# Attention with 8-wide heads: maximum products dealt one by one between scores and values, and another order of stores and loads in the first round

## What is computed

```python
x = x + _L1_attn_ref(_layernorm(x, axis=-1), ...)      # fifth branch
...
x = x + _L3_attn_ref(_layernorm(x, axis=-1), ...)      # eleventh branch

def _L1_attn_ref(x, wq, bq, wk, bk, wv, bv, wo, bo):
    q, k, v = (proj(wq, bq), proj(wk, bk), proj(wv, bv))   # 16 heads x 8
    scores = jnp.einsum('bhqd,bhkd->bhqk', q, k) * scale
    attn = jax.nn.softmax(scores, axis=-1)
    out = jnp.einsum('bhqk,bhkd->bhqd', attn, v)
    ...
    return jnp.einsum('bld,ed->ble', out, wo) + bo

def _L3_attn_ref(x, Wq, bq, Wk, bk, Wv, bv, Wp, bp, rel_bias_table):
    # as above, with rotary q and k, and before the softmax:
    att = (jnp.einsum('bhid,bhjd->bhij', q, k) + bias[None]) * (1.0 / math.sqrt(D))
    att = jnp.where(pos[None, :] <= pos[:, None], att, -jnp.inf)
```

## Time and profile before

| | us | share of the span |
|---|---|---|
| median of three runs | 3683.9 | |
| the profiled execution, its own time | 3683.4 | |
| its span | 3681.6 | 100% |
| PE busy | 3164.9 | 86% |
| PEld busy | 1625.1 | 44% |
| DVE busy | 2543.4 | 69% |
| ACT busy | 1894.4 | 51% |
| POOL busy | 1013.4 | 28% |

### The profile page before, as it was taken

One profiled execution on the slowest core, in us unless ns is written; L12 is line 12 of the kernel. 1 busy time (PEld: TensorE's weight loads), 2 busy tenths in 40 slices (PEclk: granted clock), 3 DMA queues, 4 the chain that ended last, 5 costly groups with the idle time before them and its releaser, 6 DMA issues. The chain is left out here.

```text
span 3681.6 us, 61554 instructions
## 1 busy us (share of the span) xinstructions
PE 3164.9 (86%) x23589; PEld 1625.1 (44%) x23629; DVE 2543.4 (69%) x5604; ACT 1894.4 (51%) x3454; POOL 1013.4 (28%) x860
## 2 busy tenths in 40 slices
PE   4678876799979999999889988989998688788899
PEld 3212233566642222222356666656675222222577
DVE  8787779877858888888477774464434777884433
ACT  2232222677747888888677773223222256667321
POOL 0345552767730000000187650001201201211100
PEclk9879978899988999999999999989999579899899
DMA  0000000211124000000021100001101400000100
GB/s 21 9 1 1 0 0 12 75 28 33 31 75 172 1 1 1 2 1 1 26 58 37 31 20 28 2 26 45 49 1 50 123 1 30 33 1 1 45 1 12
DMA packets 72696, 99.85 MB, mean 27 GB/s; under 512 B 11668, under 2 KB 50968, under 8 KB 72280
## 3 DMA queue, kind: packets, MB, share of 16 engines
q1 hardware_dynamic: 72408, 95.92, 8.8%
HBM read 60.18 MB, written 19.45 MB: 22 GB/s over the span
## 5 line engine op out<-in xcount | busy, mean ns | idle before, releaser
L1958 ACT ACTIVATE AR<-ps 128x1024 f32<-128x1024 f32 (+2 forms) x756 | 716.5, 997 | 175.4 <-PE ps L1861 142.0
L2041 DVE TENSOR_REDUCE AR<-ps 128x1 f32<-128x512 f32 x1056 | 689.4, 687 | 144.5 <-PE ps L1829 131.6
L1861 PE MATMUL ps<-AR 32*128 32x512 bf16 (+3 forms) x4992 | 511.9, 382 | 6.2 <-ACT AR L1958 3.1
L1829 PE MATMUL ps<-AR 32*128 32x512 bf16 (+3 forms) x1664 | 362.6, 400 | 117.9 <-DVE AR L2038 59.7
L1878 PE MATMUL ps<-AR 128*32 128x512 f32 (+3 forms) x3328 | 444.9, 608 | 5.7 <-ACT AR L1963 5.2
L2464 PEld LDWEIGHTS ps<-AR 128*128 128x128 f32 x3072 | 363.0, 192 | 60.5 <-issue 47.6
L2623 DVE SCALAR_TENSOR_TENSOR X<-ps,AR,X 128x128 f32<-128x128 f32 x512 | 143.6, 344 | 343.9 <-PE ps L2464 343.6
L2464 PE MATMUL ps<-AR 128*128 128x128 f32 x3072 | 363.2, 275 | 0.0
L1829 PEld LDWEIGHTS ps<-AR 32*128 32x128 bf16 x1664 | 94.9, 92 | 504.1 <-DVE AR L2041 241.2
L2439 PE MATMUL ps<-XT,AR 128*128 128x512 f32 x672 | 307.7, 594 | 0.1
L209 POOL TENSOR_TENSOR rs<-rs,halves 128x4 f32<-128x4 f32 x48 | 49.5, 1032 | 818.1 <-DVE rs L201 818.0
(11 more groups left out here) (324 smaller groups left out, 5718.9 us busy)
## 6 DMA issues: line engine op xcount, KB each, us to landing
AR<-AR SPq DMA_DIRECT2D x124, 128.0 KB, 2.3
AR<-in_c_rot SPq DMA_DIRECT2D x64, 128.0 KB, 2.2
AR<-in_L3f_w SPq DMA_DIRECT2D x30, 256.0 KB, 5.2
rows_KA<-AR SPq DMA_DIRECT2D x32, 128.0 KB, 2.4
AR<-scr_bias SPq DMA_DIRECT2D x32, 128.0 KB, 3.2
AR<-in_L2f_w SPq DMA_DIRECT2D x30, 128.0 KB, 2.7
AR<-rows_KC SPq DMA_DIRECT2D x7, 512.0 KB, 6.2
AR<-rows_KA SPq DMA_DIRECT2D x6, 512.0 KB, 5.1
```

The lines of the kernel that those rows point to most:

```text
L1829: e.matmul(g.bank[b][:, 0:w], QA[rows, q, 128 * i:128 * i + 128], KA[rows, q, 512 * first:512 * first + w], start=way != "kept", stop=True ...
L1861: t = e.matmul(g.bank[h][:, lo:512], K[32 * h:32 * h + 32, q, 128 * kt:128 * kt + 128], Q[32 * h:32 * h + 32, q, queries], start=y == 0, s ...
L1958: e.activation(dst[:, :, lo:512], src[:, :, lo:512], ACT.Exp, scale=self.scale).then_inc(*s.up("exp" if u else "left", k, i, *((1,) if u e ...
L2041: e.tensor_reduce(o, g.bank[b][:, 0:w], AXX, ALU.max).then_inc(*s.up("reduced", k, n, h, st, kc))
```

## The change

- **Dealing.** The maximum products of a step come one head at a time instead of in pairs of heads: with four of them, one ahead of the first scores, one between the first and the second scores, one between the second scores and V, one behind V. With more, they are spread over the four slots evenly. The scores of a step thus become two entries of the list, "score" 0 and 1; "step" remains for the engines that read it.
- **Closing.** The closing of a round stands at the end of a step, behind V and the fourth slot, instead of ahead of a finish and V.
- **Head.** "kept" and "met" go to head 1 instead of head 3.
- **Fills.** The five constant blocks are copied from a new input, `c_fill`, by five DMAs at the start of the kernel, behind the loads of X and of c_mats and ahead of the first stage's loads. The buffer, the two memsets of GpSimd and the five DMAs in the non-causal stage are gone.
- **First round.** Chunk 2 of q is made ahead of chunks 0 and 1; it is stored and loaded alone ahead of these two; chunks 0 and 1 have a signal of their own, `d_loaded7`.
- **Table.** After the last piece, ScalarE takes an exponential of one column (`warm`), in both stages.

```diff
+    c["c_fill"] = np.stack([np.full((128, 1024), 0x3F803F80, np.uint32), np.zeros((128, 1024), np.uint32)]).view(f)
...
         self.parts = [(c, j) for c in range(4) for j in (1, 0)] if causal else [
-            (0, 1), (3, 0), (1, 1), (2, 1), (3, 1), (0, 0), (1, 0), (2, 0)]
+            (0, 1), (3, 0), (1, 1), (2, 1), (3, 1), (2, 0), (0, 0), (1, 0)]
...
-        if self.causal or (n and h != 3):
+        if self.causal or (n and h != 1):
             return "alone"
...
-    def plan_max(self, n, half, st, kc):
+    def plan_max(self, n, half, st, kc, only=None):
         out = []
-        for h in (2 * half, 2 * half + 1):
+        for h in (2 * half, 2 * half + 1) if only is None else (only,):
...
             pairs = [self.next_max(half, goal, 3) for half in (1, 0)]
-            order = [x[y] for y in range(3) for x in pairs if y < len(x)]
-            if order:
-                self.plan_max(*order.pop(0))
-            self.plan.append(("step", i, n, kt, self.hold(0, ("left", i)) + self.hold(1),
-                              self.hold(2, ("exp", i, 1)) + self.hold(3)))
-            for x in order:
+            order = [x[y] + (2 * x[y][1] + z,) for y in range(3) for x in pairs if y < len(x) for z in range(2)]
+            slots = [[x for y, x in enumerate(order) if 4 * y // max(4, len(order)) == z] for z in range(4)]
+            for u in range(2):
+                for x in slots[u]:
+                    self.plan_max(*x)
+                self.plan.append(("score", i, n, kt, u, self.hold(2 * u, ("exp", i, 1) if u else ("left", i)) + self.hold(2 * u + 1)))
+            self.plan.append(("step", i, n, kt))
+            for x in slots[2]:
                 self.plan_max(*x)
             if self.rows_due:
                 self.plan_rows_max(self.rows_due.pop(0))
-            self.plan_closed()
             if finish_due:
                 self.plan_finish(finish_due.pop(0))
...
+            for x in slots[3]:
+                self.plan_max(*x)
+            self.plan_closed()
             p += area[i]
...
-            e.wait_ge(*s.at("filler", k, 1))
-            for block in (2, 3):
-                e.dma_start(g.rows["KC"][:, block, :, :], self.filler[:, 0:2048]).then_inc(*s.up("d_stored7", k, "KC", block, by=16))
-            for name, block in (("QB", 3), ("QC", 2), ("QC", 3)):
-                e.dma_start(g.rows[name][:, block, :, :], self.filler[:, 2048:4096]).then_inc(
-                    *s.up("d_stored7", k, name, block, by=16))
             self.store_all(e, s, 0, 1, chunk(0), "d_stored0")
...
             self.store_rest(e, s, 3, 1, whole, "d_stored5")
-            e.wait_ge(*s.at("third", k, 2, 0))
-            most = slice(0, 1536)
-            self.store_all(e, s, 2, 0, most, "d_stored6")
-            e.wait_ge(*s.at("d_stored7", k, "QC", 3))
+            self.store_all(e, s, 2, 0, chunk(2), "d_stored6")
+            e.wait_ge(*s.at("d_filled", "QC", 3))
             e.wait_ge(*s.at("d_stored5", k, "KC", 1, 3))
...
-            self.load(e, s, "QA", 0, most, "d_loaded6")
-            self.store_rest(e, s, 2, 0, most, "d_stored6")
-            e.wait_ge(*s.at("d_stored6", k, "QC", 1, 2))
+            self.load(e, s, "QA", 0, chunk(2), "d_loaded6")
+            self.store_all(e, s, 1, 0, slice(0, 1024), "d_stored7")
+            self.store_rest(e, s, 1, 0, slice(0, 1536), "d_stored7")
+            e.wait_ge(*s.at("d_stored7", k, "QC", 1, 1))
+            most = slice(0, 1536)
+            self.load(e, s, "QA", 0, slice(0, 1024), "d_loaded7", "a")
             self.load(e, s, "QB", 0, most, "d_loaded7", "b")
             self.load(e, s, "QC", 0, most, "d_loaded7")
...
                 e.activation(self.P[:, j, 1, chunk(c)], self.RC[:, y % 3, :], ACT.Copy).then_inc(*s.up("piece", k, c, j, 2))
+                if y == len(self.parts) - 1:
+                    e.activation(self.warm[:, 0:1], self.bqk[:, 0:1], ACT.Exp)
...
-            e.memset(self.filler[:, 0:2048], 1.0).then_inc(*s.up("filler", k, 0))
-            e.memset(self.filler[:, 2048:4096], 0.0).then_inc(*s.up("filler", k, 1))
...
     e.dma_start(g.C[:, :], g.I["c_mats"]).then_inc(*s.up("d_c", by=16))
+    for name, block, x in (("KC", 2, 0), ("KC", 3, 0), ("QB", 3, 1), ("QC", 2, 1), ("QC", 3, 1)):
+        e.dma_start(g.rows[name][:, block, :, :], g.I["c_fill"][x].bitcast(BF16).rearrange("(h d) n -> h d n", h=16)).then_inc(
+            *s.up("d_filled", name, block, by=16))
     for stage in stages:
         stage.sync(e, s)
```

More of the change, by code:

```diff
@@ L1446, in allocate @@
         self.junk = ar.bf16(2, 512)
+        self.warm = ar.f32(2)
         if causal:
@@ L1454, in allocate @@
         self.PB = ar.f32(4, 1024)
-        self.filler = self.PB.rearrange("p a b -> p (a b)").bitcast(BF16)
         assert not causal or ar.at <= 41500 - 9216
@@ L1667, in max_rows_in @@
             return "d_loaded%d" % c
-        return "d_loaded4" if c == 3 else "d_loaded6"
+        return "d_loaded4" if c == 3 else "d_loaded6" if c == 2 else "d_loaded7"
     def score_rows_in(self, gr, c, key):
@@ L1846, in tensor @@
                 t.then_inc(*s.up("m_turned", k, n))
-            if what == "step":
-                i, n, kt, old0, old1 = x
+            if what == "score":
+                i, n, kt, u, old = x
                 (gr, qc), lo = self.rounds[n], self.low(n, kt)
                 q, queries = gr % self.slots, slice(512 * qc + lo, 512 * qc + 512)
[L1851 to L1862, removed]
-                    t.then_inc(*s.up("scored", k, i, u))
+                self.wait_left(e, s, old)
+                if u == 0 and kt == 0:
+                    e.wait_ge(*s.at("max_row", k, n))
+                name = self.score_rows_in(gr, kt // 4, True)
+                if name not in seen:
+                    seen.add(name)
+                    e.wait_ge(*s.at(name, k))
+                for y, (K, Q) in enumerate(((KA, QA), (KA, QB), (KC, QC))):
+                    for h in (2 * u, 2 * u + 1):
+                        t = e.matmul(g.bank[h][:, lo:512], K[32 * h:32 * h + 32, q, 128 * kt:128 * kt + 128],
+                                     Q[32 * h:32 * h + 32, q, queries], start=y == 0, stop=y == 2, skip_group_check=True)
+                t.then_inc(*s.up("scored", k, i, u))
             if what == "values":
@@ L1938, in scalar @@
             if what == "step":
-                i, n, kt, _, _ = x
+                i, n, kt = x
                 near, lo = self.near_cols(n, kt), self.low(n, kt)
@@ L2084, in gpsimd @@
         g, k = self.g, self.k
-        if not self.causal:
-            e.memset(self.filler[:, 0:2048], 1.0).then_inc(*s.up("filler", k, 0))
-            e.memset(self.filler[:, 2048:4096], 0.0).then_inc(*s.up("filler", k, 1))
         e.memset(self.MN.rearrange("p a b c -> p (a b c)"), 0.0).then_inc(*s.up("m_cleared", k))
@@ L2667 @@
     "d_expert%d" % i for i in range(8)) + tuple("d_low%d" % i for i in range(6)) + tuple(
-        "d_loaded%d" % i for i in range(14))
+        "d_loaded%d" % i for i in range(14)) + ("d_filled",)
 SHARED = {
     "v_setup": ("halves", "identb", "cleared", "q_scale", "band", "x_cleared", "o_cleared", "masked", "offset_scale", "selection"),
-    "g_setup": ("taps_cleared", "k_padded", "v_padded", "k_cleared", "v_cleared", "m_cleared", "filler", "ones"),
+    "g_setup": ("taps_cleared", "k_padded", "v_padded", "k_cleared", "v_cleared", "m_cleared", "ones"),
     "router": ("logits", "compared", "rank", "mass", "chosen", "gates"),
```

## The result

The changed kernel takes 3650.0 us (median of four runs, 3643.0 to 3656.7) against 3683.1 before; the ratio is 0.9908, its 95% interval 0.9887 to 0.9930. It is **faster by 33 us**, where 3687 was forecast and 3666 was the lower end. The profiled execution of after took 3656.7, its span is 3654.9 against 3681.6; it is the slowest of the four.

What follows compares the result with a forecast made beforehand. First-stage steps were bound by a three-bank loop of maximum product, reduce, next products and V. Terms -9.2 + 4.5 + 6.4 - 4.5 + 3 + 2.6 = +2.8 gave 3686.2, stated as 3687; range 3666 to 3702.

Steps and rivals of the forecast that it cites:

- The step that failed: Causal stage: steps with eight or more maxima are paced by VectorE, eight reduces taking 5.1 before and after.
- Net 2.6 lost: Causal stage in sum: 2.9 gained in regular steps, 5.5 lost at finish and maximum row; bounds 8 gained, 11 lost.
- Rival 2: Causal stage: shorter TensorE waits bring a third of the low-clock time back to 2.4 GHz; 20 less, 3667; chance 0.18.
- Rival 1: First attention stage: VectorE's four reduces become the loop if over 0.65 apart; 12 slower, 3699; chance 0.18.
- The first stage's steps: First attention stage: regular pairs 5.06 against 5.16, 9.2 gained; finish 4.5 lost, maximum row 6.4 lost.
- The kept step: First attention stage: step in which head 1's maximum product is kept, with a Relu of 0.61; claimed to take 2.61.
- The maximum row: First attention stage, 14 times: row waits for the closing behind V, starts at 2.20 instead of 1.45; 6.4 lost.
- The first round: Start of the first attention stage: earlier K stores 2.4, chunk 2 of Q 2.1; 4.5 gained, bounds 0 and 5.5.
- Chunk 2: First attention stage, round 1: storing and loading it alone removes the product's wait for negated Q rows, 2.1 gained.
- GpSimd's two memsets hid behind the normalisation: Ahead of the first attention stage's products: removing these memsets was given no gain.
- The fills at the start: Kernel start: copies delay weights; 0.3 lost at the stores' rate (landing 15.7), 7.9 at half, nothing if faster; 3 taken.
- Rival 3: Kernel start: fills run at half the stores' rate, 7.9 lost instead of 3; 3692; chance 0.09.

Runs made afterwards that it cites:

- mended row in both stages: The changed kernel with, in both stages, the step's last products and the closing ahead of V where they complete a round's maxima: 3640.1 us, ratio 0.9887.

## Why the prediction was wrong, and where it was right

**The step that failed** is the causal stage: "Steps with eight or more maxima are VectorE's: eight reduces are 5.1 either way". The row behind it, was read for its 5.12 and not for the 2.42 of idle time that stands on the same line. The eight reduces are 5.1 either way; what VectorE waits ahead of and between them is not. The prediction reads waits in the first stage alone; the same view of the causal stage, which it does not use, has 82.7 us of VectorE waiting for TensorE and 83.6 the other way. Two engines that wait for each other by turns leave neither busy all the time (385 of 518 for VectorE), and this was taken for slack of the stage instead of its bound. Net 2.6 lost was forecast, with 8 gained as the bound; 27.7 were gained.

**Rival 2** had the sign and the stage, but it put the gain down to a clock that comes back, which was the smaller part. The clock rose from 0.86 to 0.88 in that execution, up to 0.92 in others, and by the estimate above a fifth to a half of the gain goes with it. What was held against it, "VectorE, at 393 of 530 busy, holds the crowded steps", is the same mistake. Rival 1 did not come: reduces in a row stand some 0.6 apart in the first stage (three take 1.88 to 1.94), under its 0.65, and the kept step is 2.60.

**The first stage's steps** came out as worked out, except for sizes. Timeline of after, a step that ends a round, with its finish, and the next, TensorE:

```profile
1344.94 1.07 PE L1877 MATMUL ps<-AR 128*32 128x512 f32 x8
1345.94 0.39 PE L1829 MATMUL ps<-AR 32*128 32x512 bf16 x2
...
1347.72 0.66 PE L1886 MATMUL ps<-C,AR 128*128 128x128 f32 x4 [0.22 <-DVE AR L2042]
1348.31 1.07 PE L1877 MATMUL ps<-AR 128*32 128x512 f32 x8
...
1350.91 1.07 PE L1877 MATMUL ps<-AR 128*32 128x512 f32 x8
...
1353.40 1.06 PE L1877 MATMUL ps<-AR 128*32 128x512 f32 x8
```

The kept step is 2.60 (1348.31 to 1350.91; forecast 2.61), the met one 2.49 (forecast 2.45; the hop is 0.05, and the met pass with its read of the accumulator takes 0.70 instead of 0.68), so the pair 5.09, not 5.06. The transposes start 1.78 after the step's first product (forecast 1.87), and the step is 3.37 (3.46). The maximum row:

```profile
1334.44 0.39 PE L1829 MATMUL ps<-AR 32*128 32x512 bf16 x2
...
1335.67 0.22 DVE L2048 TENSOR_REDUCE AR<-AR 128x16 f32<-128x64 f32 x1
...
1336.67 0.10 PEld L1841 LDWEIGHTS ps<-AR,identb 128*128 128x128 bf16 x1 [0.97 <-DVE AR L2042]
```

From M1, the first of the two at 1334.44, to the row's load at 1336.67 it is 2.23 (forecast 2.20), the step 3.79 (3.75). Where 1.7 was forecast the rounds cost 5.4 (from the first V to the end of the stage 680.0 before, 685.4 after): 0.31 in each of 13 rounds, and 0.7 and 0.6 in the first and the last but one. The pairs gave two thirds of their 9.2, 5.17 to 5.10; a row step costs 0.48 and a finish 0.20.

**The first round** gave 4.7 (65.84 to 61.10), and 4.5 was forecast, by terms that do not hold; that the sums meet is luck. Chunk 2 was worth 0 and not 2.1, though the prediction itself named VectorE's passes as what is late next. The fills were worth some 2 where 2.4 was forecast. Some 0.9 is the clock of that execution, as the two groups above show. The dealing gave 0.8 (from the first product to V 35.81 in the kernel with pairs in the first stage, 35.00 in the changed one) and the table load 0.4. Some 0.7 is left for the memsets and the sources of the copies. The first two K stores, of which the prediction says that they met full rings, took 1.64 and 1.57 to issue before and 0.58 and 0.60 after; what held them no run shows.

"GpSimd's two memsets hid behind the normalisation" is not what the traces have. The second group of four of VectorE's normalisations, before and after:

```profile
1072.95 3.85 DVE L216 TENSOR_SCALAR XN<-X,mv,rs 128x128 f32<-128x128 f32 x4 [0.29 <-POOL rs L209]
```
```profile
1074.93 1.92 DVE L217 TENSOR_SCALAR XN<-X,mv,rs 128x128 f32<-128x128 f32 x4 [0.29 <-POOL rs L210]
```

With the two memsets gone it takes half the time (1.96 with the fills late). What of this reaches the first product is not shown.

**The fills at the start** cost 0.05 and not 3. VectorE's first weight pass:

```profile
15.46 1.32 DVE L234 TENSOR_REDUCE AR<-AR 128x70 f32<-128x1120 f32 x1
```

It was at 15.41. That the weights wait for the fills was right; the price was wrong. In the trace the fills' packets, of 32 KB each, run from 5.7 to 13.1: 2.62 MB in 7.4 us, 356 GB/s, so the rate was near that of the stores (342) and not between it and its half. Rival 3, half of it, did not come. The weights, 0.54 MB, had landed at 7.9 before; now their first packet starts at 12.2, when the last of the fills has started, and the last ends at 14.8. DMA of after from 12.2 to 14.9 us:

```profile
DMA packets 960, 0.54 MB, mean 200 GB/s; under 512 B 128, under 2 KB 960, under 8 KB 960
```

So the weights came 6.9 later and 0.6 ahead of the pass that needs them; by the first of the prediction's three estimates they would have come at 15.7, 0.3 too late. In the kernel with the mended row in both stages (3640.1 us) they landed at 15.7, and there the pass did wait:

```profile
15.98 1.32 DVE L234 TENSOR_REDUCE AR<-AR 128x70 f32<-128x1120 f32 x1 [0.62 <-DMA AR<-in_L_ffn_w_down]
```

The Trainium skill's page DMA: Bandwidth & Descriptors (section Latency and other measured facts) gives 207 to 214 GB/s for copies between HBM tensors. This trace, with 356, does not agree with that figure, and the loss worked out by it, 5.1, did not come.

## What to carry to other kernels

Where two engines feed each other through a small ring of banks, deal the work in the smallest pieces that have a wait of their own: two products issued together behind two waits give the consumer nothing until the second bank is free. With own waits the order around V mattered less here, some 3 us from V to V for each part; with pairs, one pair behind V cost 73. Before a stage is called one engine's, read the waits in both directions in that stage, and the idle time on the very line from which a duration is taken. Where work moves behind V, see what its followers (here the closing and the maximum row) lose by it, and give the step that completes a round an order of its own. Where two executions differ in clock, compare the steps that ran at the same granted clock in both.

## What the runs showed of the hardware

A stage whose order of work was identical took 485 to 496 us in six kernels, and its granted clock went with it, 0.92 to 0.88; on the 104 of its 159 steps that ran at the full clock in all six, the times agree within 0.5 us. A gain in such a stage needs more than one profile of each side, or such a comparison.

Five copies of 0.52 MB from HBM to HBM moved at 356 GB/s (7.4 us), and the loads issued behind them moved behind them, 6.9 us later than without. VectorE saw 0.05 of it, because it needed the weights only at 15.4; in one of the other kernels it did wait.

Four normalisations of VectorE took 3.85 us beside GpSimd's memsets, and 1.92 with two of these gone.
